# A two-layer pair kernel: the right sums move into gate's and left's banks, ScalarE takes them out, y is handed over behind its crossed part, one root visit fewer

## What is computed

```python
# layer 0
x = layernorm(pair, ln1_w, ln1_b)
left  = sigmoid(x @ left1)  * (x @ left2)
right = sigmoid(x @ right1) * (x @ right2)
p = einsum('nsre,nkre->nske', left, right)
p = layernorm(p, ln2_w, ln2_b)
g = sigmoid(einsum('nsrz,zy->nsry', x, gate))
x1 = pair + einsum('nrse,ez->nsrz', p, out_w) * g
# layer 1
left  = x1 @ W_left + b_left + x1 @ W_eq + b_eq
right_sum = sum(x1 @ W_right + b_right, axis=2, keepdims=True)
gate  = sigmoid(x1 @ W_gate + b_gate)
y = (left * right_sum * gate) @ W_out + b_out + x1
return layernorm(y, ln_scale, ln_bias)
```

## Time and profile before

| | before |
|---|---|
| median of 3 runs | 102.99 us (102.9 to 103.06) |
| the profiled execution | 103.13 us |
| its span | 101.2 us |
| TensorE, VectorE, ScalarE, GpSimd busy | 79.8, 69.9, 66.0, 53.0 us |
| moved by DMA | 4.68 MB |

### The profile page before, as it was taken

One profiled execution on the slowest core, in us unless ns is written; L12 is line 12 of the kernel. 1 busy time (PEld: TensorE's weight loads), 2 busy tenths in 40 slices (PEclk: granted clock), 3 DMA queues, 4 the chain that ended last, 5 costly groups with the idle time before them and its releaser, 6 DMA issues.

```text
span 101.2 us, 3184 instructions
## 1 busy us (share of the span) xinstructions
PE 79.8 (79%) x1260; PEld 59.9 (59%) x1260; DVE 69.9 (69%) x285; ACT 66.0 (65%) x107; POOL 53.0 (52%) x69
## 2 busy tenths in 40 slices
PE   0997999789999999999789897999999658650000
PEld 0984887667878899744336584766767427540000
DVE  0477699846375800198899999999899975399500
ACT  0643967998877266689784999489668997631000
POOL 5138994799920050006295409754097099978200
PEclk9999999999999999999999999999999999999555
DMA  3999998000000000000000000000002406438996
GB/s 47 194 153 145 147 147 83 12 10 12 0 0 0 3 6 0 0 0 0 0 0 10 3 6 0 6 0 6 0 0 43 67 6 101 65 55 134 146 146 96
DMA packets 34079, 4.68 MB, mean 46 GB/s; under 512 B 33936, under 2 KB 34064, under 8 KB 34064
## 3 DMA queue, kind: packets, MB, share of 16 engines
q1 hardware_dynamic: 32304, 4.10, 32.5%
q10 hardware_dynamic: 1760, 0.38, 2.0%
HBM read 2.38 MB, written 2.10 MB: 44 GB/s over the span
## 4 chain that ended last, share of the span: by engine, by line
PE 39%; DVE 20%; ACT 19%; issue 10%; POOL 5%; DVEq 0%; POOLq 0%; ACTq 0%
PE bank L846 10%; PE bank L909 7%; ACT L435 5%; ACT L574 5%; PE bank L853 4%; PE bank L919 3%; PE bank L831 3%; DVE x1T L724 3%; DVE st L739 3%; PE bank L1008 3%; POOL xc L313 2%; DVE stats L602 2%; DVE stats L681 2%; DVE u L715 2%; DVE lr L617 2%
## 5 line engine op out<-in xcount | busy, mean ns | idle before, releaser
L374 POOL TENSOR_TENSOR t_tok<-p_sb,rstd 128x512 f32<-128x512 f32 x7 | 10.1, 1451 | 12.2 <-DVE rstd L687 11.0
L846 PE MATMUL bank<-lr_blk,xnT 64*128 64x256 f32 x128 | 15.6, 388 | 0.7 <-ACT xnT L446 0.7
L617 DVE TENSOR_TENSOR lr<-bank,sig_lr 128x512 f32<-128x512 f32 x16 | 10.9, 682 | 6.5 <-ACT sig_lr L455 6.4
L846 PEld LDWEIGHTS bank<-lr_blk,xnT 64*128 64x128 f32 x128 | 11.8, 186 | 3.2 <-issue 1.2
L383 POOL TENSOR_TENSOR oT<-o_a,rsum 128x512 f32<-128x512 f32 x8 | 8.3, 1040 | 10.2 <-DVE o_a L733 10.2
L681 DVE BATCH_NORM_STATS2 stats<-p_sb 128x6 f32<-128x64 f32 x64 | 8.6, 215 | 6.9 <-ACT p_sb L499 6.9
L455 ACT ACTIVATE sig_lr<-bank 128x512 f32<-128x512 f32 x16 | 9.5, 597 | 3.3 <-PE bank L846 3.1
L602 DVE BATCH_NORM_STATS2 stats<-x_tok 128x6 f32<-128x64 f32 x64 | 9.0, 212 | 0.8 <-DMA x_tok<-in_x 0.7
L724 DVE SCALAR_TENSOR_TENSOR x1T<-bank,w_rep,u 128x128 f32<-128x128 f32 x32 | 9.3, 346 | 0.1
L403 POOL TENSOR_TENSOR sq<-lr,row_rep 128x512 f32<-128x512 f32 x6 | 8.3, 1386 | 1.4 <-DVE lr L757 0.6
L435 ACT ACT_TABLE_LOAD x7 | 9.0, 1283 | 0.1
(11 more groups left out here) (99 smaller groups left out, 170.7 us busy)
## 6 DMA issues: line engine op xcount, KB each, us to landing
x_tok<-in_x SPq DMA_DIRECT2D x14, 128.0 KB, 4.2
out<-sq SPq DMA_DIRECT2D x7, 256.0 KB, 3.6
x_tok<-in_x SPq DMA_DIRECT2D x3, 64.0 KB, 3.2
w_rep<-in_weights ACTq DMA_DIRECT2D x4, 45.1 KB, 3.2
out<-sq ACTq DMA_DIRECT2D x1, 128.0 KB, 3.8
out<-sq SPq DMA_DIRECT2D x1, 128.0 KB, 4.7
x_tok<-in_x ACTq DMA_DIRECT2D x1, 64.0 KB, 2.6
scale_rep<-in_rows SPq DMA_DIRECT2D x1, 64.0 KB, 8.9
```

What stands on the lines that cost most here:

```text
L374: nc.gpsimd.tensor_tensor(t_tok[:, c % 2], by_token(p_sb[:, :, s]), by_token(rstd[:, 1:2, s]).to_broadcast([P, SPC, CH]), ALU.mult).then_i ...
L617: nc.vector.tensor_tensor(lr[:, :, s].rearrange("p f (b q) -> p b f q", q=GRP), src[:, :, 2 * CH:4 * CH], sig_lr[:, j % 3].rearrange("p (b ...
L846: last = nc.tensor.matmul(dst, xnT[half, c, k * P:(k + 1) * P], lr_blk[half], start=True, stop=True, skip_group_check=True)
```

## The change

- The right sums of chunks 0 to 6 are put into the columns of GL in which left will lie, those of chunk 7 into Q. `project_sums(c)` therefore waits for o_a(c-1), and `project_1(c)` for rsum(c).
- `project_crossed(c)` raises y's semaphore itself, for every chunk.
- rsum is computed by ScalarE (Identity with a bias), behind the square of the iteration, one iteration earlier than VectorE did.
- The roots of chunks 1, 2 and 3 are taken together at i = 7; the visit at i = 8 is gone. At i = 9 the table load is brought on ahead of the wait for y. The reciprocal of chunks 1 to 3 stands ahead of weigh in iteration 8.
- Chunk 3 is scaled by VectorE in place of GpSimd, and chunk 4's bias goes from VectorE to GpSimd.
- At the start of the second half, the first right sums stand behind q(1) and the second input transposes; the reciprocals of the second layernorm stand one step later on VectorE.

Cut to its core:

```diff
-ROOTS3 = [(0, 1), (1, 3), (3, 4), (4, 6), (6, 7), (7, 8)]
-ROOT3_AT = {5: [0], 7: [1], 8: [2], 9: [3]}
-INVERSE3_AT = {6: [0], 8: [1], 9: [2]}
+ROOTS3 = [(0, 1), (1, 4), (4, 6), (6, 7), (7, 8)]
+ROOT3_AT = {5: [0], 7: [1], 9: [2]}
+INVERSE3_AT = {6: [0], 8: [1]}
 BIAS_FIRST = {8: [1]}
-BIAS_AT = {6: [0], 8: [2], 9: [3]}
-ON_VECTOR = (4, 5, 6, 7)
-ON_POOL = (0, 1, 2, 3)
-OWN_BIAS = 4
+BIAS_AT = {6: [0], 8: [2]}
+ON_VECTOR = (3, 4, 5, 6, 7)
+ON_POOL = (0, 1, 2)
...
         def sums_bank(c):
-            return Y if c else Q
+            return GL if c < CHUNKS - 1 else Q
...
+            def sums_of_right(c):
+                act.wait_ge(rs_ps, c + 1)
+                b = sums_bank(c)
+                nc.scalar.activation(two(rsum[:, c]), bank[:, b:b + 2, HALF:HALF + 2], ACT.Identity, bias=right_bias[:]
+                                     ).then_inc(rs_ready, 1)
...
                 if i == CHUNKS + 1:
+                    nc.scalar.activation(scratch[:, 2:3], eps[:], ACT.Sqrt)
                     evacuate_y(i - 3)
...
+                if 0 <= i - 1 < CHUNKS:
+                    sums_of_right(i - 1)
-                if i == 3 or i in ROOT3_AT and i <= CHUNKS:
+                if i == 3 or i in ROOT3_AT and i < CHUNKS:
                     nc.scalar.activation(scratch[:, i:i + 1], eps[:], ACT.Sigmoid)
...
             for i in range(CHUNKS + 2):
-                if i == 2:
-                    sums_of_right(0)
                 if 0 <= i - 1 < CHUNKS:
                     residual0(i - 1)
-                if 0 <= i - 2 < CHUNKS and i > 2:
-                    sums_of_right(i - 2)
+                if i == 1:
+                    inverse2(1)
+                if i == 4:
+                    inverse2(2)
+                for b in INVERSE3_AT.get(i, []):
+                    inverse3(b)
                 if 0 <= i - 4 < CHUNKS:
                     weigh3(i - 4)
                 if 0 <= i - 1 < CHUNKS:
                     residual1(i - 1)
-                for b in INVERSE3_AT.get(i, []):
-                    inverse3(b)
...
             def project_sums(c):
                 pe.wait_ge(x1_ready, BLK * (c + 1))
-                if c == 1:
-                    pe.wait_ge(g_ready, GATE0_ORDER.index(7) + 1)
-                elif c > 1:
-                    pe.wait_ge(y_crossed, c - 1)
+                if c:
+                    pe.wait_ge(oa_ready, c if c < CHUNKS - 1 else 1)
+                else:
+                    pe.wait_ge(g_raw, 2)
...
-                last.then_inc(y_ps if c > 1 else rs_ps, 1)
+                last.then_inc(rs_ps, 1)
...
+                if c < CHUNKS - 1:
+                    pe.wait_ge(rs_ready, c + 1)
...
-                project_tiles(c, Y, wout_blk, 1).then_inc(y_crossed if c + 2 < CHUNKS else y_ps, 1)
+                project_tiles(c, Y, wout_blk, 1).then_inc(y_ps, 1)
...
-            project_sums(0)
             project_q(1)
             transpose_x(1)
+            project_sums(0)
```

More of the change, by code:

```diff
@@ L203, in pair_layers @@
         out_scaled, ys_ps = sem("out_scaled"), sem("ys_ps")
-        y_straight, y_crossed, ys_straight = sem("y_straight"), sem("y_crossed"), sem("ys_straight")
+        y_straight, ys_straight = sem("y_straight"), sem("ys_straight")
         last_half, half_out = sem("last_half"), sem("half_out")
-        scaled, scaled_pool, final, final_vector = sem("scaled"), sem("scaled_pool"), sem("final"), sem("final_vector")
+        scaled, scaled_pool, final = sem("scaled"), sem("scaled_pool"), sem("final")
         TT, XT, Q, GL, Y = 0, 1, 2, 4, 6
@@ L282, in _ @@
                 s = slice(c * SPC, (c + 1) * SPC)
[L283 to L286, removed]
+                sp.wait_ge(final, c + 1)
                 sp.dma_start(out_tok_dram[:, s, :], sq[:, s, :]).then_inc(x_out, 16)
@@ L418, in _ @@
                     bias3(c)
-            for c in (5, 6):
+            for c in (3, 4, 5, 6):
                 bias3(c)
@@ L551, in _ @@
                     nc.scalar.activation(scratch[:, 1:2], eps[:], ACT.Sigmoid)
+                    act.wait_ge(biases, 3)
                 if i < CHUNKS:
@@ L556, in _ @@
                     gate0(6)
-                if i == 2:
-                    act.wait_ge(biases, 3)
                 if 0 <= i - 2 < CHUNKS:
@@ L571, in _ @@
                     evacuate_y(i - 3)
-                if i == 3 or i in ROOT3_AT and i <= CHUNKS:
+                if 0 <= i - 1 < CHUNKS:
+                    sums_of_right(i - 1)
+                if i == 3 or i in ROOT3_AT and i < CHUNKS:
                     nc.scalar.activation(scratch[:, i:i + 1], eps[:], ACT.Sigmoid)
-            for b in (4, 5):
+            for b in (3, 4):
                 root3_of(b)
@@ L698, in _ @@
             statistics2(4)
[L699 to L710, removed]
             def residual0(c):
@@ L789, in _ @@
                     gated1(i - 2)
-                if i == 3:
-                    inverse2(2)
                 if 0 <= i - 4 < CHUNKS:
                     variance3(i - 4)
-            inverse3(3)
-            scale3(4)
-            variance3(6)
-            scale3(5)
-            s = slice(OWN_BIAS * SPC, (OWN_BIAS + 1) * SPC)
-            dve.wait_ge(scaled, ON_VECTOR.index(OWN_BIAS) + 1)
-            nc.vector.tensor_tensor(sq[:, s, :], yn[:, s, :], row_rep[:, 1:2, :].to_broadcast([P, SPC, CH]),
-                                    ALU.add).then_inc(final_vector, 1)
-            variance3(7)
-            inverse3(4)
+            scale3(3)
+            variance3(6)
+            inverse3(2)
+            scale3(4)
+            scale3(5)
+            variance3(7)
+            inverse3(3)
             dve.wait_ge(rstd3, len(ROOTS3) - 1)
@@ L806, in _ @@
             normalise3(6, 1).then_inc(scaled, 1)
-            inverse3(5)
+            inverse3(4)
             lo = (CHUNKS - 1) * SPC
@@ L1025, in centre_y @@
                 if c == 0:
-                    pe.wait_ge(rs_ready, 2)
+                    pe.wait_ge(g_ready, GATE0_ORDER.index(7) + 1)
                 elif c < CHUNKS - 1:
@@ L1075, in _ @@
                     pe.wait_ge(out_scaled, 2)
+                    pe.wait_ge(rs_ready, CHUNKS)
                     centre_scaled_y(CHUNKS - 2)
```

1 line of the change is left out of this document (removed).

## The result

The changed kernel takes **101.89 us** (median of 4 runs, 101.74 to 102.03), the kernel before 102.97 beside it. The ratio is 0.9895, with an interval of 0.9877 to 0.9912: faster by 1.08 us, where 2.2 were forecast. The direction is right and the time lies in the range, but half of the gain is missing. The profiled execution took 101.74 us, 1.39 less than that of before. Some 0.14 of it stands in the profiles before anything that was edited: q(0) on TensorE, the first product with the output weights, before (the first row) and in the changed kernel (the second).

What follows compares the result with a forecast made beforehand. The output transfer stream sets the end, 10.84 us after chunk 3's issue, which VectorE's order and GpSimd's queue decide. 1.72 + 1.13 - 0.65 = 2.20 us gained, median 100.8 from 102.99; range 99.9 to 102.8.

Steps and rivals of the forecast that it cites:

- The reciprocal: VectorE's reciprocal for chunks 1 to 3, moved ahead of weigh, starts GpSimd's queue earlier: 1.72 us freed, less d.
- The rival in which the root is late: Root of chunks 1 to 3 late, VectorE stalls; 1 us miss gives 101.8; 0.14 together with the dear rsum.
- d: How much later o_a(6) ends on VectorE through the new waits: 0.65 us forecast, bounds 0 and 2.8.
- the first two terms: Start of d: gate(1) waiting for rsum(1) behind three gate sigmoids, +0.68; q(1) moved into a TensorE wait, -0.25.
- The dear rsum: Rival: rsum holds ScalarE 0.60 like a full tile, d 2.53, median 102.7; 0.14 together with the stalled reciprocal.
- the ring: Rival: sums, rsum and hops add 0.59 to each of six turns, d 3.54, median 103.7, slower; chance 0.12.
- scale(3): Scaling chunk 3 on VectorE takes 1.13 us off GpSimd's queue, at no VectorE cost behind variance 5.
- the stream's 1.80: Time in us of one 256 KB output chunk in the closing transfer stream at 146 GB/s.
- The stream rule: Span ends 10.84 us after chunk 3's issue if chunks 4 to 7 come at least one per 1.80 us.
- More than forecast: Rival: earlier y and lighter VectorE give back all of d, bias(3) runs uncontended: 99.8; chance 0.10.
- The early y: y handed over behind its crossed part: only shortens ScalarE's idle time; the square's waits in visits counted within d.
- The visit left out: Root visit at i = 8 removed: no term in the sum; if kept, o_a(7) would be 0.74 too late.

## Why the prediction was right or wrong

- **The reciprocal: right.** It starts at 79.05 and scale(1) at 79.58, inside the 79 to 80 foretold, and GpSimd's wait before oT(6) ends with o_a(6). Taking only this back costs 1.4 us. The rival in which the root is late did not come: the root waited 0.24 for the variance of chunk 3 and VectorE none for the root.
- **d, the lateness of o_a(6): 0.80, not 0.65**, and 0.94 with the two profiles lined up at q(0). It ends at 81.54 + 0.75 = 82.29, against 81.49. Most of the miss is at the start: at sig(1) the first two terms made 0.68 - 0.25 = 0.43, and it is 59.09 - 58.43 = 0.66. ScalarE's row of before:

```profile
58.43 0.69 ACT L535 ACTIVATE sig<-bank,gate_bias 128x512 f32<-128x512 f32 x1
```

  rsum(1) did start 0.23 before 57.76, but 0.14 of that is the earlier execution. gate(1) started 0.41 behind rsum's start, not 0.26: the row took 0.26, not 0.22, and in each of the four waits TensorE started 0.14 to 0.15 after its end, where a hop of 0.04 was counted. And the 57.34 of gate(1) is from the chain; the timeline of before has it at 57.27. gate(1) came near the 58.02 named as a sign because the earlier start and the longer handover cancel in part. Moving rsum(1) alone gives 0.57 back (0.68 foretold). An rsum holds ScalarE 0.15, not 0.13. The dear rsum and the ring did not come: TensorE waited four times, not in every turn.
- **scale(3): the term was mis-sized.** 1.13 was taken as free, but oT(7) on GpSimd took 1.49 beside scale(3) on VectorE, 0.45 back. Against that, bias(3), which now began ahead of scale(4), took 1.27 where 1.60 was kept, 0.33 forward. With d these make 0.15 + 0.45 - 0.33 = 0.27 of the 0.31 by which chunk 3 was late.
- **The step that failed: that chunk 4 follows chunk 3 within the stream's 1.80.** "That is under the stream's 1.80 and costs nothing at the end" was said of chunk 4's bias, moved to GpSimd behind bias(3), by the duration of the piece alone. But that piece needs scale(4), and scale(4) on VectorE was shut out while bias(3) ran. So bias(4) began 0.63 late and took 1.64, beside scale(5). The chunks came 2.28 apart, 0.48 more than 1.80, and the end came 11.33 behind chunk 3, 0.49 more than 10.84. What is shown of this is the price of bias(3) beside scale(4): without it chunk 4, and the end with it, come 1.0 to 1.1 earlier. The place of chunk 4's bias alone, which the sentence was about, is not shown to cost anything in the median. The stream rule itself held where its condition did: with chunk 4 at 1.67 to 1.75 and the later ones close behind, three kernels ended 10.86 to 11.05 behind chunk 3; with chunk 4 at 2.27 or 2.28, five ended 11.32 to 11.63 behind it.
- **The rows of before already had it.** bias(3) at 88.74 took 1.60 beside a 1.27 for the same work. Under "More than forecast" the prediction lets bias(3) run "uncontended", but it took the two durations for bounds and did not ask what the longer one ran beside. VectorE's timeline of before has it:

```profile
88.24 0.97 DVE L757 TENSOR_TENSOR lr<-lr,rstd 128x512 f32<-128x512 f32 x1
...
89.73 1.16 DVE L757 TENSOR_TENSOR lr<-lr,rstd 128x512 f32<-128x512 f32 x1
```

  scale(4) began beside GpSimd's scale(3), which ran until 88.66, and took 0.97; bias(3) began beside scale(4) and took 1.60; scale(5) began beside bias(3) and took 1.16. Alone this form takes 0.69. Slow rows on two engines at the same times, each behind the other's, are not spread, but one resource.
- **The early y: the price was wrong, the end not.** "Where no visit lies this shortens only ScalarE's idle time, since the next sigmoid hangs on o_a and not on y" overlooks that rsum was put behind the square on ScalarE. The part is worth 0.7 us as long as rsum stands there; no run has the late y with rsum on VectorE. As the sum held neither this loss nor this gain, it came out even.
- **The visit left out: right as a cover.** The prediction gave it no time of its own; without it the whole gain is lost.
- **Profile and median.** The profiles differ by 1.39 us and the medians by 1.08. The working accounts for the profile: 2.20 foretold, 0.31 lost by chunk 3's issue, 0.49 behind it. The other 0.3 is where the two profiled executions lie in their runs; 0.14 of it is there at q(0).

The parts taken back one at a time cost 1.4, 1.0, 0.7 and 0.4 us, far more than the 1.08 that all of them gained. So they don't add: each is worth that beside the others, and the change also cost d. Which of the two weighs more is not shown.

## What to carry to other kernels

Before a piece is moved to an engine "under cover", look at what its input's producer runs beside, and not only at how long the piece is: here VectorE and GpSimd took turns, and the price showed on the engine that started second. A duration that comes in two sizes in a trace asks for the row that stands beside the longer one on the other engines. Where a stream of transfers sets the end, check the spacing of every issue, not the first issue alone. Two profiles are lined up at a row ahead of the edit before their times are compared: here they differed by up to 0.3 us there, as much as some of the effects.
